# Two-layer MoE block on Trainium2: rows sent to their experts by quarters, with extra waits between the scatters

## The reference

```python
# layer 0
h = x @ W0[subject[segment]] + b0[subject[segment]]          # 16 subjects, 128x128
logits = h @ w_router.T                                       # 16 experts, the largest one is taken
s = sigmoid(logits[top])
gate, up = split((s * h) @ gate_up[top])                      # 2 x 256
x = x + (silu(h @ w_gate.T) * (h @ w_up.T)) @ w_down.T + (up * silu(gate)) @ down[top]
# layer 1
a = x + relu(x @ W1[lang] + b1[lang]) @ W2[lang] + b2[lang]   # 10 languages
h = layernorm(a) * gamma[lang] + beta[lang]
gates = softmax(h @ router_w)                                 # 8 experts, two per token
# top-2 gating with capacity 1280 rows per expert: a first choice's place is the count of earlier
# first choices of its expert; a second choice's place starts behind all first choices of the expert
x = x + sum_k g_k * (silu(h @ w1[e_k] + b1[e_k]) @ w2[e_k] + b2[e_k]) + 0.1 * shared(h)
```

## Time and profile before

| | |
|---|---|
| median of 3 runs | 536.86 us (533.89 to 537.79) |
| the profiled execution | 532.79 us, span 531.0 us |
| mean granted TensorE clock | 0.939 of full |
| busy share of the span | PE 84%, DVE 45%, ACT 47%, POOL 48% |
| bytes moved by DMA | 57.96 MB |

### The profile page before, as it was taken

How to read it: one execution, slowest core, us unless ns; L and a number is a source line. 1 busy time by engine, 2 the same in 40 slices (tenths; PEclk the granted TensorE clock), 3 DMA queues, 4 the chain that set the end, 5 groups by cost and what they waited for, 6 DMA issues and landing times.

```text
span 531.0 us, 9984 instructions
## 1 busy us (share of the span) xinstructions
PE 447.7 (84%) x3129; PEld 384.3 (72%) x3130; DVE 240.2 (45%) x708; ACT 247.4 (47%) x593; POOL 256.3 (48%) x272
## 2 busy tenths in 40 slices
PE   6798879965999998899997879918999999999900
PEld 4698746644777775477786869908999999999800
DVE  1344486422555554244868865212333233323237
ACT  2234486202555553356456534403555555555424
POOL 3003567771555555500246777760555555655510
PEclk8989999996999999899999799977999999999965
DMA  9999921111322220800001111113234324331169
GB/s 255 398 308 356 393 63 45 55 50 46 78 71 68 78 64 8 237 10 2 11 30 42 45 51 46 55 40 100 66 116 123 107 68 141 109 79 34 35 175 307
DMA packets 66131, 57.96 MB, mean 109 GB/s; under 512 B 9485, under 2 KB 53152, under 8 KB 66099
## 3 DMA queue, kind: packets, MB, share of 16 engines
q1 hardware_dynamic: 58402, 43.99, 27.7%
q0 software_dynamic: 7168, 12.51, 7.3%
q10 hardware_dynamic: 528, 1.05, 0.5%
HBM read 30.28 MB, written 29.47 MB: 113 GB/s over the span
## 4 chain that ended last, share of the span: by engine, by line
PE 63%; POOL 12%; issue 12%; DVE 5%; DMA 5%; ACT 1%; POOLq 1%; SPq 0%; DVEq 0%; ACTq 0%
PE PS L1459 13%; PE PS L1145 8%; POOL rows L568 7%; PE PS L1189 6%; PE PS L1381 4%; POOL rows L536 4%; PE PS L1268 4%; PE PS L1447 4%; PE PS L1448 4%; PE PS L1449 4%; PE PS L1253 2%; PE PS L1255 2%; PE PS L1254 2%; PE PS L1368 2%; PE PS L1206 2%
## 5 line engine op out<-in xcount | busy, mean ns | idle before, releaser
L586 POOL DMA_INDIRECT back<-grp_y,grp_i x80 | 79.6, 996 | 71.9 <-DVE grp_y L1102 58.0
L568 POOL DMA_INDIRECT rows<-disp,slot x64 | 64.9, 1014 | 66.8 <-DVE slot L946 47.2
L1459 PE MATMUL PS<-w2r,act 128*128 128x128 f32 x640 | 77.7, 275 | 0.0
L1459 PEld LDWEIGHTS PS<-w2r,act 128*128 128x128 f32 x640 | 74.7, 191 | 0.0
L735 ACT ACTIVATE act<-PS,b1r 128x256 f32<-128x256 f32 x160 | 62.8, 475 | 14.5 <-PE PS L1449 14.5
L547 POOL DMA_INDIRECT back<-act,blk_i x48 | 47.0, 980 | 42.0 <-DVE act L906 21.3
L1102 DVE TENSOR_TENSOR grp_y<-PS,b2r 128x256 f32<-128x256 f32 x40 | 17.0, 425 | 89.3 <-PE PS L1459 84.4
L596 ACT ACTIVATE xh<-PS 128x256 fp32r<-128x256 f32 (+1 forms) x48 | 20.0, 418 | 74.2 <-PE PS L1145 74.2
L1447 PE MATMUL PS<-xh,w1h 128*128 128x256 f32 x160 | 48.3, 302 | 0.0
L526 POOL TENSOR_TENSOR w_gul<-w_raw,w_guh 128x512 fp32r<-128x512 f32 x16 | 21.0, 1336 | 50.1 <-ACT w_guh L596 50.1
L1448 PE MATMUL PS<-xl,w1h 128*128 128x256 f32 x160 | 44.9, 281 | 0.0
(11 more groups left out here) (216 smaller groups left out, 946.0 us busy)
## 6 DMA issues: line engine op xcount, KB each, us to landing
rows<-zrow SPq DMA_DIRECT2D x32, 258.0 KB, 5.4
grp_x<-rows SPq DMA_DIRECT2D x40, 129.0 KB, 2.3
w_raw<-in_f_gate_up SPq DMA_DIRECT2D x8, 512.0 KB, 7.7
back<-zrow SPq DMA_DIRECT2D x8, 512.0 KB, 6.9
back<-back SPq DMA_DIRECT2D x16, 256.0 KB, 4.6
blk_x<-rows SPq DMA_DIRECT2D x48, 64.5 KB, 1.8
acc<-in_x SPq DMA_DIRECT2D x8, 256.0 KB, 5.2
y0g<-back SPq DMA_DIRECT2D x8, 256.0 KB, 3.2
```

What stands on the lines that cost most here:

```text
L568: gp.indirect_dma_start(rows1, bass.IndirectOffsetOnAxis(ap=slot[:, k, t:t + 1], axis=0), disp[:, t, :], None, bounds_check=E1 * CAP - 1, ...
L586: gp.indirect_dma_start(back1, bass.IndirectOffsetOnAxis(ap=grp_i[v % NX][:, u:u + 1], axis=0), grp_y[k][:, u, :], None, bounds_check=last ...
L1459: last = mm(PS[5 + k][:, u * P:(u + 1) * P], act[k][:, c, u * P:(u + 1) * P], w2r[e][:, c, :], start=c == 0, stop=c == C1 - 1)
```

## The change

- **Layer 0, slots by quarters.** Ranks are worked out for eight tiles at a time. `first_expert(r)` at the end of stages 2, 4, 6, 8; PE's `rank0(r)` in the midst of the subject matmuls of stages 3, 5, 7, and the last after `shared0_up(0)`; DVE's `read_rank(r)` and `page_slots(r)` in the same stages, and for r = 3 ahead of `glu0(0)`. An expert's rows lie in pages of 128, and a quarter takes new pages when the last one is full; so slots no longer depend on later counts. The page table for PE comes by a comparison over partitions and one matmul (`pe_bx`).
- **The score travels as a column** of the row (`ROW` is 130, not 129): `disp` isn't scaled any more, and gate and up are multiplied by the score in the experts' `silu` and `glu`. A buffer `blk_x` is free after `glu`, so `load_block` waits for `e_ac` in place of `e_xt` and `e_ix`.
- **`w_gul`** is made by DVE (`low_half`, two per group of the shared expert, behind `add0`), not by POOL. `rows0` is filled with zeros ahead of the weights' loads.
- **Layer 0's scatters** go out by quarters; up to tile 23, each four tiles wait until the four before have landed.
- **Layer 1, both choices by quarters.** `second_choices(r)` at the end of stages 5, 7, 9 and after the loop; one `rank1` and one `quarter_slots` for both choices, in stages 6, 8, 10 and after the loop. Second choices are numbered from the expert's end downwards, in a buffer of their own, `rows1b`, which is filled with zeros too (20 more fills). The softmax moves behind, and ACT's Exp behind `shared1_silu(2)`.
- **Layer 1's scatters** go out as eight tiles to `rows1`, eight to `rows1b`, and so on; each eight wait until the eight before have landed.
- **Groups** are loaded from both buffers and merged on DVE by `q_merge` (two instructions a group), on which `q_tr` waits.

```diff
-    ROW = H + 1
+    ROW = H + 2
...
+    rows1b = nc.dram_tensor("rows1b", (E1 * CAP, ROW), fp32).ap()
...
+            for r in range(E0 // 2):
+                sp.dma_start(w_raw[:, r * 2 * F0x2:(r + 1) * 2 * F0x2].rearrange("p (e f) -> p e f", e=2),
+                             f0_gate_up[2 * r:2 * r + 2].rearrange("e p f -> p e f")).then_inc(g_ld[r], 16)
...
-                             zrow[:, 0:zw]).then_inc(zero1, 16)
+            for rows in (rows1, rows1b):
+                for r in range(0, E1 * CAP, P * 4):
+                    sp.dma_start(rows[r:r + P * 4, :].rearrange("(p a) r -> p (a r)", p=P),
+                                 zrow[:, 0:zw]).then_inc(zero1, 16)
             for r in range(0, TOP_K * T, P * 8):
...
-                    sp.wait_ge(e_xt, j - 3)
-                    sp.wait_ge(e_ix, j - 3)
+                    sp.wait_ge(e_ac, j - 3)
...
                 sp.dma_start(grp_x[k][:, :, :], at(rows1_q, m)).then_inc(gx_ld[k], 16)
+                sp.dma_start(grp_z[k][:, :, :], at(rows1b_q, m)).then_inc(gx_ld[k], 16)
...
-            for e in range(E0):
-                cols = slice(e * F0x2, (e + 1) * F0x2)
-                pool.wait_ge(g_hi, e + 1)
-                gp.tensor_tensor(w_gul[:, cols], w_raw[:, cols], w_guh[:, cols].bitcast(fp32),
-                                 ALU.subtract).then_inc(g_lo, 1)
...
             for t in range(NT):
-                if t % (NT // 2) == 0:
-                    pool.wait_ge(slots0, t // (NT // 2) + 1)
-                if t % G == 0:
-                    pool.wait_ge(scaled, t + G)
+                if t % RT == 0:
+                    pool.wait_ge(slots0, t // RT + 1)
+                    pool.wait_ge(scored, t // RT + 1)
+                    pool.wait_ge(tok_done, (t + RT) // G)
+                if t % G == 0 and 0 < t < NT - RT:
+                    pool.wait_ge(sc0[(t // G - 1) % 2], 16 * G * ((t // G - 1) // 2 + 1))
                 gp.indirect_dma_start(rows0, bass.IndirectOffsetOnAxis(ap=slot[:, 0, t:t + 1], axis=0),
                                       disp[:, t, :], None, bounds_check=NBLKP * P - 1,
-                                      oob_is_err=False).then_inc(sc0, 16)
+                                      oob_is_err=False).then_inc(sc0[t // G % 2], 16)
...
+            for r in range(NR):
+                pool.wait_ge(slots1, r + 1)
+                pool.wait_ge(b_tk, (r + 1) * RT // G)
+                for k, rows in ((0, rows1), (1, rows1b)):
+                    if k == 1:
+                        pool.wait_ge(sc1[0], 16 * RT * (r + 1))
+                    elif r > 0:
+                        pool.wait_ge(sc1[1], 16 * RT * r)
+                    for t in range(r * RT, (r + 1) * RT):
+                        gp.indirect_dma_start(rows, bass.IndirectOffsetOnAxis(ap=slot[:, k, t:t + 1], axis=0),
+                                              disp[:, t, :], None, bounds_check=E1 * CAP - 1,
+                                              oob_is_err=False).then_inc(sc1[k], 16)
...
+            def sigmoid(r):
+                eng.wait_ge(mx0, r + 1)
+                sc.activation(disp[:, r * RT:(r + 1) * RT, H + 1], m1[:, r * RT:(r + 1) * RT],
+                              ACT.Sigmoid).then_inc(scored, 1)
...
+                    if n >= 3 and n % 2 == 1:
+                        sigmoid((n - 3) // 2)
...
-                for t in range(n * 2 * G, min((n + 1) * 2 * G, NT)):
-                    sc.activation(disp[:, t, 0:H], disp[:, t, 0:H], ACT.Copy,
-                                  scale=score[:, t:t + 1]).then_inc(scaled, 1)
...
+            def silu(j, k, s):
                 eng.wait_ge(e_gu, j + 1)
-                sc.activation(blk_s[k][:, :], PS[k][:, 0:F0], ACT.Silu).then_inc(e_sl, 1)
+                sc.activation(blk_s[k][:, :], PS[k][:, 0:F0], ACT.Silu,
+                              scale=blk_x[s][:, H + 1:H + 2]).then_inc(e_sl, 1)
...
+            def first_expert(r):
+                first_max(lg, E0, t1, own(mask, r).rearrange("p e i -> p i e"), r * RT, RT)
+                v.engine_nop().then_inc(mx0, 1)
+                both = slice(r * KQ, (r + 1) * KQ)
+                link(v.tensor_tensor_scan(seen[:, both], rst1[:, :], mask[:, both], 0.0, ALU.mult, ALU.add))
+                v.engine_nop().then_inc(mk0, 1)
...
+            def read_rank(r):
+                dve.wait_ge(pe_rank0, r + 1)
+                total, later = (page[0], page[7])[r % 2], (page[7], page[0])[r % 2]
+                link(v.tensor_tensor(later, total, PS[6][:, 3 * P:3 * P + E0], ALU.add))
+                link(v.tensor_tensor(et(rank, RT), et(PS[6][:, 2 * P:3 * P], RT), bc(total.unsqueeze(2), over), ALU.add))
+                v.engine_nop().then_inc(rk0, 1)
+            def page_slots(r):
+                later = (page[7], page[0])[r % 2]
+                held, holds = (page[1], page[5])[r % 2], (page[5], page[1])[r % 2]
+                end, before_end = (endE, padF)[r % 2], (padF, endE)[r % 2]
+                at_old, at_new, gap, fresh = page[2], page[3], page[4], page[6]
+                link(v.tensor_scalar(padI[:, :], later, float(P - 1), None, ALU.add))
+                link(v.tensor_scalar(padI[:, :], padI[:, :], P.bit_length() - 1, P.bit_length() - 1,
+                                     ALU.arith_shift_right, ALU.arith_shift_left))
+                link(v.tensor_copy(holds, padI[:, :]))
+                link(v.tensor_tensor(fresh, holds, held, ALU.subtract))
+                if r == 0:
+                    link(v.tensor_tensor_scan(end[:, :], ones_f[:, :], fresh, 0.0, ALU.mult, ALU.add))
+                else:
+                    link(v.tensor_tensor_scan(gap, ones_f[:, :], fresh, 0.0, ALU.mult, ALU.add))
+                    link(v.tensor_scalar(end[:, :], gap, before_end[:, E0 - 1:E0], None, ALU.add))
+                link(v.tensor_tensor(at_new, end[:, :], holds, ALU.subtract))
+                if r > 0:
+                    link(v.tensor_tensor(gap, at_old, at_new, ALU.subtract))
+                    link(v.tensor_tensor(et(older, RT), et(rank, RT), bc(held.unsqueeze(2), over), ALU.is_lt))
+                    link(v.tensor_tensor(et(older, RT), et(older, RT), bc(gap.unsqueeze(2), over), ALU.mult))
+                    link(v.tensor_tensor(rank, rank, older, ALU.add))
+                link(v.tensor_tensor(et(rank, RT), et(rank, RT), bc(at_new.unsqueeze(2), over), ALU.add))
+                link(v.tensor_tensor(rank, rank, mask[:, r * KQ:(r + 1) * KQ], ALU.mult))
+                link(v.tensor_reduce(slotF[:, 0, r * RT:(r + 1) * RT], by_t(rank, RT), AX.X, ALU.add))
+                v.tensor_copy(slot[:, 0, r * RT:(r + 1) * RT], slotF[:, 0, r * RT:(r + 1) * RT]).then_inc(slots0, 1)
+                link(v.tensor_tensor(startE[:, r * E0:(r + 1) * E0], end[:, :], fresh, ALU.subtract))
+                if r == 0:
+                    link(v.tensor_copy(at_old, at_new))
+                elif r < NR - 1:
+                    link(v.scalar_tensor_tensor(out=gap, in0=fresh, scalar=0.0, in1=gap, op0=ALU.is_gt, op1=ALU.mult))
+                    link(v.tensor_tensor(at_old, at_old, gap, ALU.subtract))
             for n in range(NG + 1):
...
                                     ALU.add).then_inc(hT_done, 1)
+                if n >= 3 and n % 2 == 1:
+                    read_rank((n - 3) // 2)
                 if n < NG:
...
+                if n >= 3 and n % 2 == 1:
+                    page_slots((n - 3) // 2)
...
+            read_rank(NR - 1)
+            page_slots(NR - 1)
             glu0(0)
...
+            def low_half(e):
+                cols = slice(e * F0x2, (e + 1) * F0x2)
+                dve.wait_ge(g_hi, e + 1)
+                v.tensor_tensor(w_gul[:, cols], w_raw[:, cols], w_guh[:, cols].bitcast(fp32),
+                                ALU.subtract).then_inc(g_lo, 1)
...
+                for e in (2 * n - 2, 2 * n - 1):
+                    low_half(e)
...
+            def glu(j, k, s):
                 dve.wait_ge(e_sl, j + 1)
-                v.tensor_tensor(blk_a[k][:, :], PS[k][:, F0:F0x2], blk_s[k][:, :], ALU.mult).then_inc(e_ac, 1)
+                v.scalar_tensor_tensor(out=blk_a[k][:, :], in0=PS[k][:, F0:F0x2], scalar=blk_x[s][:, H + 1:H + 2],
+                                       in1=blk_s[k][:, :], op0=ALU.mult, op1=ALU.mult).then_inc(e_ac, 1)
...
+            def second_choices(r):
+                cols = quarter(r)
+                one, two = (chosen(mask, r, k).rearrange("p e i -> p i e") for k in range(TOP_K))
+                link(v.tensor_tensor(te(t1[:, cols], E1), te(lg[:, cols], E1),
+                                     bc(m1[:, r * RT:(r + 1) * RT].unsqueeze(2), [P, RT, E1]), ALU.subtract))
+                link(v.scalar_tensor_tensor(out=te(t2[:, cols], E1), in0=one, scalar=-BIG, in1=te(t1[:, cols], E1),
+                                            op0=ALU.mult, op1=ALU.add))
+                link(v.tensor_scalar(t2[:, cols], t2[:, cols], FLOOR, None, ALU.max))
```

(60 more changed lines are left out.)

325 lines of the change are left out of this document (154 added, 171 removed).

## The result

The changed kernel took 556.69 us in the median of four runs (553.27 to 559.10), the kernel before, run beside it, 535.38 in the median of four: a ratio of 1.0475, with a 95% interval of 1.0326 to 1.0624. The profiled execution took 553.27 (span 551.2), 20.5 more than that of the kernel before. The prediction was 554.6.

What follows compares the result with a forecast made beforehand. Bound by PE, with stretches where scatters, not matmuls, set the end. Layer 0 +3.5 and layer 1 +14.2 give +17.7 on a median of 536.86: 554.6 us; forecast's own range 548 to 561 (50%), 80% range 540 to 563.

Steps and rivals of the forecast that it cites:

- The first loop: Layer 0, stages 3 and 5: page work covered by subject matmuls; three `rank0` and late copies cost 1 us.
- DVE's page work in stage 7: Layer 0: `page_slots(2)` has no cover there, so `featT` comes 4.8 us later, at 72.2, PE idle 4.6.
- The clock behind it, and the second gap: Layer 0: half rate after idleness costs up to 2 us each time; PE idles 5.8 before `shared0_up(1)`, at 85.2.
- The tail: Layer 0's end: last shared-expert sum at 127.2, then two `low_half` of 0.69 each; blocks start at 129.3.
- The clock's give-back of 1.5 in the blocks: Layer 0's blocks: PE idles only 2.2 before them, so they start at full rate, giving back 1.5 us.
- The rival of late block loads: Layer 0's blocks: loads stall PE by up to 0.3 us in most of 48 blocks, total 564.6; chance 8%.
- Layer 1's first scatter: Layer 1: quarter 0's slots come in stage 6, not 5, so the first scatter starts at 271.1, not 261.70.
- The waits: Layer 1's scatters: seven waits between batches, 3.28 us each from start to start, 14.0 us of the added time.
- The term for slower scatters: Layer 1: a scatter's mean of 1.014 us against the undisturbed 0.98 adds 2 us in all.
- The rival of cheap waits: Layer 1: POOL resumes early enough, batches cost as little as unbroken ones; layer 1 adds 0.2, total 540.6; chance 12%.
- the one of faster small batches: Layer 1: scatters in small batches run at 0.98 us each, so layer 1 loses 19, total 535.7; chance 8%.
- Groups at the same pace: Layer 1's 40 groups: the 39 later merges have a stage of slack each and cost nothing.

Runs made afterwards that it cites:

- the second execution: The changed kernel run again, unaltered, on chip B beside the kernel before: 555.80 us, ratio 1.0443.
- experiment 6: Changed kernel with last two quarters' page work moved, low halves early, no layer-1 waits: 528.97 us on B, 590.54 on C; with waits kept, 544.71 on B.
- Experiment 3: Changed kernel with the last two quarters' page arithmetic moved behind the shared expert's products, six low halves later, on chip A: 544.95 us, ratio 1.0215.
- experiment 4: Kernel before plus a wait for the landing of each eight layer-1 scatters, on chip A: 542.55 us, ratio 1.0200.
- experiment 2: Changed kernel without the waits after every four scatters of layer 0, on chip A: 556.66 us, ratio 1.0454.
- experiment 1: Changed kernel without the waits between layer 1's eight batches of eight scatters, on chip A: 541.86 us, ratio 1.0155.

## Why the prediction was right

The range held, and the forecast case came true; the sizes that made it are these, by its own steps.

- **The first loop**: given 1, with 0 to 2. It ended 1.2 later than before in the profiled execution and at the same time in the second. But over the seven traces of the changed kernel and its variants on A, B and the first chip it ended at 64.8 to 68.7, 66.7 in the mean, against 64.7 and 63.7 in the two traces of the kernel before and its variant. So the term was too small on the whole. Where the rest comes from was not followed up.
- **DVE's page work in stage 7**: right. `page_slots(2)` from 66.7, `featT` done at 72.27, predicted 72.2; PE idle 4.45, predicted 4.6.
- **The clock behind it, and the second gap**: right. Clock 0.50 after both; `shared0_up(1)` at 85.35, predicted 85.2. Its price was somewhat too low: the step gave 4 us of work at half rate, and behind the second pause the windows show it from 85.35 to about 91 (86 to 90 has 0.50, 90 to 92 has 0.73), 5.7 us of work, an estimated 2.9 in place of 2.0. Nor did it take over 3 us of idleness: the clock fell after the 2.29 ahead of the blocks too, and once with a pause of 1.93 (experiment 6). Experiment 3 shows that it is the place of the links, not their sum on DVE: moved, they gave back 10.1 of "shared".
- **The tail**: right. Last sum 128.30, predicted 127.2; blocks at 130.55, predicted 129.3. Of the 1.1 of the sum, 0.9 is that price of the clock. In the second execution the sum is at 127.27 and the blocks begin at 129.56, nearly as predicted, but by luck: the first loop took 1 less than the prediction gave it, the clock 0.9 more.
- **The clock's give-back of 1.5 in the blocks**: wrong. The step said that 2.2 of idleness would leave the blocks at full rate. They began at it, but the clock fell at 132 all the same: ahead of the blocks PE had idled 0.87, 2.29 and some more between transposes. Instead of shrinking by 1.5, "blocks" was 84.4 in three of four executions of the unchanged part, and 85.3 in the profiled one, whose fifth block waited 1.39 for its load; before it was 83.8, and 85.1 in the variant of experiment 4, which is the same in layer 0. So it neither grew nor shrank clearly. That the clock does stay up behind a shorter pause, and then gives back about 1, is in the traces of experiment 6. Layer 0 as a whole, with the first loop, grew by 7.8 in the profiled execution (1.2 + 5.1 + 1.5) and by 5.9 in the second one (0.1 + 5.3 + 0.6, from the table and the ends of the first loop, rounded), where 3.5 was predicted. The rival of late block loads did not occur beyond that one wait.
- **Layer 0's scatters hidden**: right, by experiment 2. The first was issued at 41.55, predicted 42, the last at 106.97.
- **Layer 1's first scatter**: right. 9.4 later predicted; 8.0 in the profiled execution, 9.4 in the second one.
- **The waits**: right in kind, by experiments 1 and 4. 3.28 each predicted, 3.06 to 3.34 measured. The term for slower scatters, 2.0, was 0.4 in the profiled execution and 2.1 in the second. The rival of cheap waits falls (12.5 back when they go), and so does the one of faster small batches: the pace in a batch is 1.286.
- **The merge**: 1.2 predicted, 1.4 measured. PE's gap ahead of `q_tr(0)` was 21.17, predicted near 24. Layer 1 in all 10.8 profiled and 14.0 in the second execution; predicted 14.2.
- **Groups at the same pace**: nearly. The step that 39 merges have a stage of slack failed at one place. The timeline of DVE:

```profile
407.30 0.61 DVE L1182 SCALAR_TENSOR_TENSOR grp_x<-grp_z,second,grp_x 128x129 f32<-128x129 f32 x2
412.08 0.42 DVE L1202 TENSOR_TENSOR grp_y<-PS,b2r 128x256 f32<-128x256 f32 x1 [4.18 <-DMA back<-grp_y,grp_i]
...
413.89 0.61 DVE L1182 SCALAR_TENSOR_TENSOR grp_x<-grp_z,second,grp_x 128x129 f32<-128x129 f32 x2
```

DVE stood in `q_result`'s wait for a late store (6.42 from issue to landing by the chain of waits), the merge behind it came late, and PE idled 1.43 for it at 414.55. This was no accident of one execution: in all seven traces of the changed kernel and its variants from A, B and the first chip DVE waits 3.8 to 4.4 there, and PE then 1.1 to 1.7 for the merge. In the two traces of the kernel before and its variant DVE never waits more than 2.5 for a store, and PE's `q_tr`, which waited for the load alone, doesn't idle behind it. Why the store is so late in the changed kernel is open. The column "groups" grew by 0.6 to 2.2 over the executions.

The sum, 17.7 against 20.5 (21.3 in the medians), is close partly by luck, because the errors have both signs: for the profiled execution layer 0 was 4.3 too small, layer 1 was 3.4 too large, and 1.6 came from the groups and the end.

The Trainium skill ("DMA: Bandwidth & Descriptors", Anatomy of one DMA) gives 2.15 as an estimate for the landing of such a scatter, nearly all of it completion. The landings behind the batches were 2.28 to 2.54 in the chain of waits of the changed kernel, 0.1 to 0.4 more. That the next scatters hide a landing if nobody waits for it is shown by experiment 1, with its pace of 1.29.

## What to carry to other kernels

Sixteen to eighteen links of 0.2 to 0.3 us on an engine that is half idle cost little beside matmuls (at most 3.6 us of idleness for the two pages of experiment 3), and 4 to 5 us each plus a slow clock where the tensor engine waits for the next thing behind them: look at what stands behind an added chain on its engine, in the stage where the cover ends, and move the chain, not the work. Starting a transfer earlier helps only if nothing else became the last to arrive; here the last of layer 0's scatters went out 13 us sooner than before, for a start that DVE had put off. And measure a change that alters how densely a queue is fed on more than one chip: here the waits cost 13 us on two chips, and on a third the two kernels with them were 19 and 25 us faster than the one without.

## What the runs showed of the hardware

- A wait for the landing of eight scatters on GpSimd costs 1.9 us over the pace of 1.29; 64 scatters without a wait keep the pace of eight (A and B).
- The granted clock fell to 0.50 with PE pauses of 4.45, 5.42 and 4.21 us. It stayed at 1.00 over pauses of 1.92 and 1.65 in one execution, and fell to 0.50 after one of 1.93 in another.
- On chips C and D the engines stood still for up to 20.0 us at a time, with "remote" as the releaser, while scatters ran without waits for landings; in the two traces on C with such waits it was at most 9.8. The blocks of layer 0 took 91 to 94 there instead of 83 to 85 in every kernel.
